# Experts of an early-fusion block: turning and copying the next unit's rows earlier inside a unit

## What is computed

```python
logits = x @ gate_w.T + gate_b
top_vals, top_idx = jax.lax.top_k(logits, TOP_K)          # TOP_K = 2 of 8 experts
routing = jax.nn.softmax(top_vals)
for e in range(E):
    h = x @ w1[e].T + b1[e]                                # 512 -> 1024
    x_glu, x_lin = h[:, 0::2], h[:, 1::2]
    y = x_glu * jax.nn.sigmoid(1.702 * x_glu) * (x_lin + 1.0)
    ye = y @ w2[e].T + b2[e]                               # 512 -> 512
    we = jnp.sum(routing * (top_idx == e), axis=-1)
    out = out + ye * we[:, None]
```

## Time and profile before

| what | value |
|---|---|
| median of 3 runs | 1779.68 us (1773.2 to 1782.53) |
| span of the profiled execution, first to last instruction | 1771.3 us |
| profiled execution's own device time | not listed on its own; the three runs are 1.9 to 11.2 us over the span |
| PE busy over the span | 1334.8 us (75%) |
| DVE, ACT, POOL busy | 1275.3, 774.9, 494.2 us |
| experts, from the first first-product to the last second product | 1295.01 to 1741.85 us of the span, a quarter of it |
| chain that ended last, by line | L1930 16%, L1942 8%, L1914 1% |

### The profile page before, as it was taken

How to read it: one execution, slowest core, us unless ns; L and a number is a source line. 1 busy time by engine, 2 the same in 40 slices (tenths; PEclk the granted TensorE clock), 3 DMA queues, 4 the chain that set the end, 5 groups by cost and what they waited for, 6 DMA issues and landing times. The chain is left out here.

```text
span 1771.3 us, 30260 instructions
## 1 busy us (share of the span) xinstructions
PE 1334.8 (75%) x10236; PEld 761.7 (43%) x10236; DVE 1275.3 (72%) x2068; ACT 774.9 (44%) x1498; POOL 494.2 (28%) x312
## 2 busy tenths in 40 slices
PE   0366447838999999999999922147389999999993
PEld 0335122303444444444444300025367777777772
DVE  7976999968888888888888559998734444444441
ACT  3565313314676767777777710012033333333331
POOL 4000326742333433433200012213012332332321
PEclk9987668857999999999999965666589999999997
DMA  4002016785676677677554334416388878878855
GB/s 150 1 0 68 19 46 206 238 190 141 189 203 190 189 202 200 186 202 204 138 95 80 114 126 85 65 43 188 121 303 274 280 258 269 283 257 266 275 159 143
DMA packets 115662, 294.31 MB, mean 166 GB/s; under 512 B 19772, under 2 KB 54332, under 8 KB 105446
## 3 DMA queue, kind: packets, MB, share of 16 engines
q1 hardware_dynamic: 89262, 205.79, 37.9%
q0 software_dynamic: 25280, 84.95, 18.2%
q10 hardware_dynamic: 1056, 2.79, 0.5%
HBM read 206.39 MB, written 92.16 MB: 169 GB/s over the span
## 5 line engine op out<-in xcount | busy, mean ns | idle before, releaser
L1410 ACT ACTIVATE pT<-p 128x512 f32<-128x512 f32 x800 | 421.1, 607 | 168.1 <-PE p L1312 166.0
L1384 DVE TENSOR_REDUCE mxa<-p 128x1 f32<-128x512 f32 x640 | 409.3, 682 | 96.0 <-PE p L1294 96.0
L1294 PE MATMUL p<-ks,qs 96*128 96x512 bf16 x640 | 252.7, 398 | 32.6 <-DMA vs<-d_v 29.5
L1312 PE MATMUL p<-qs,ks 128*128 128x512 bf16 x640 | 245.0, 383 | 29.6 <-DMA qs<-nmT 17.6
L1330 PE MATMUL p<-pT,vs 128*32 128x128 f32 (+1 forms) x2560 | 205.5, 439 | 1.0 <-ACT pT L1410 1.0
L1930 PE MATMUL p<-x,w 128*128 128x256 bf16 x1728 | 191.6, 273 | 0.0
L1930 PEld LDWEIGHTS p<-x,w 128*128 128x128 bf16 x1728 | 169.1, 98 | 23.4
L1901 POOL DMA_INDIRECT d_acc<-yo,slot_row x54 | 86.6, 1603 | 310.8 <-DMA d_acc<-yo,slot_row 266.1
L2009 DVE SCALAR_TENSOR_TENSOR sg<-p,b,sg 128x256 f32<-128x256 f32 x108 | 52.3, 484 | 118.2 <-ACT sg L1975 118.2
L1330 PEld LDWEIGHTS p<-pT,vs 128*32 128x32 f32 x2560 | 66.8, 109 | 151.2 <-issue 108.4
L1265 POOL CAST xT<-xT 128x2048 bf16<-128x2048 f32 x24 | 45.3, 1887 | 297.9 <-PE p L1330 285.9
(11 more groups left out here) (340 smaller groups left out, 2073.9 us busy)
## 6 DMA issues: line engine op xcount, KB each, us to landing
w<-d_w SPq DMA_DIRECT2D x18, 2048.0 KB, 8.5
d_w<-xT POOLq DMA_DIRECT2D x24, 1024.0 KB, 6.4
shared<-d_w SPq DMA_DIRECT2D x9, 2048.0 KB, 8.5
w<-d_w SPq DMA_DIRECT2D x18, 1024.0 KB, 7.2
xT<-in_w1T POOLq DMA_DIRECT2D x16, 1024.0 KB, 10.7
qs<-d_q SPq DMA_DIRECT2D x192, 80.0 KB, 3.6
ks<-d_k SPq DMA_DIRECT2D x192, 80.0 KB, 3.7
d_v<-xT SPq DMA_DIRECT2D x20, 512.0 KB, 4.4
```

Of the source, the lines that this page charges most:

```text
L1294: mm = pe.matmul(out, qs[u][0:STACK, h, q], ks[u][0:STACK, h, 0:512], start=True, stop=True)
L1312: mm = pe.matmul(out, ks[u][:, h, k], qs[u][:, h, 0:512], start=True, stop=True)
L1384: dve.tensor_reduce(mxa[u][:, h, qt:qt + 1], bank, AX.X, ALU.max, negate=True).then_inc(s_mfree, 1)
L1410: act.activation(dst, ps[:, second_bank(c, s)], ACT.Exp).then_inc(s_p, 1)
```

## The change

`turn` moves to the place behind the second of the four first-product blocks, and `copy_rows` on ACT and DVE to the place behind the third. No instruction's shape, buffer or semaphore changes. The unit that runs last still has no turn.

```diff
@@ tensor
                     mm.then_inc(s_g1, 1)
-                if not last:
-                    turn(i, c + 1)
+                    if o == 1 and not last:
+                        turn(i, c + 1)
                 pe.wait_ge(s_w[c][1], 16 * (i + 1))
@@ scalar
                     act.copy(y[c][:, o, 0], yf[o % 2][:]).then_inc(s_yh, 1)
-                if n + 1 < NU:
-                    copy_rows(n + 1)
+                    if o == 2 and n + 1 < NU:
+                        copy_rows(n + 1)
```

## The result

| | before | changed |
|---|---|---|
| median of 4 runs | 1779.83 us (1773.2 to 1782.53) | 1820.85 us (1817.03 to 1825.42) |
| ratio, 95% interval | | 1.0227 (1.0197 to 1.0258) |
| profiled execution: span | 1771.3 us | 1823.4 us (device time 1825.42) |
| experts, first first-product to last second product | 1295.01 to 1741.85: 446.8 us | 1303.76 to 1793.84: 490.1 us |

The change made the kernel 2.3% slower, some 41 us, where 5 us were forecast; the time lies outside the range. (The two spans are 52 us apart, since the profiled execution was the fastest of its runs before and the slowest after.) Of these 52 us, 43.3 arose in the experts. The other 8.8 are in stages ahead of them, whose code is the same: in the nine profiled executions of this study the experts began between 1295.0 and 1306.4 us, and the one of before is the earliest.

What follows compares the result with a forecast made beforehand. PE was taken as the bound, waiting for nothing at 16.55 us a unit. Late-gather stalls of 1.7, 1.1, 1.0, 0.5 and 0.7 made 5 us, all else 0: 1779.7 + 5 = 1784.7 us, range 1777 to 1800.

Steps and rivals of the forecast that it cites:

- What bounds the kernel; no wait to remove: In the experts PE is busy 429.01 of 429.01 us and waits for nothing, so reordering cannot gain time.
- Copies 0, switches 0: Copies moved on ACT and DVE delay no second products, and one more PE switch per unit costs nothing: 0 us.
- The turn's wait for the gather is the cost, in units at the start and the end: On PE, the earlier turn waits for the next unit's gathered rows in some first and last units: 5 us.
- A few units at the start and some at the end are late, the middle is not: Before any shift, unit 2's gather is 0.8 us late, unit 23's 1.1 late, unit 10's has 0.8 to spare.
- The landing shifts by 0.89 us: First-product weights go out 0.89 us later, so gathers land 0.89 later: units 2, 23, 10 late by 1.7, 2.0, 0.1.
- A stall frees POOL from the weights, so stalls end themselves: Stalls let scatters lead the weights, so gathers go earlier; first units' stalls run 1.7, 1.1, 1.0, 0.5 us.
- The gathers stay late: Rival, chance 0.27: scatters stay behind the weights and the turn waits in every unit, 16 us, 1796 us.
- A stall costs the clock too: Rival, chance 0.08: four stalls each slow PE's next first products by 1.43 us, 5.7 us on top, 1790.4 us.

## Why the prediction was wrong, point by point

- *What bounds the kernel; no wait to remove.* Right: without late rows the time is that of before (ratios 1.0007 and 0.9985).
- *Copies 0, switches 0.* Right, by the run with the turn alone and by the one with the sooner gather, which has the whole change and no loss.
- *The turn's wait for the gather is the cost, in units at the start and the end.* Right in kind. The Trainium skill's rule on issuing early and waiting late (page "DMA: Bandwidth & Descriptors", section "Rules for kernel authors") named the same wait; here it cost 32.2 us of idle time in 16 units, not only at the two ends.
- *A few units at the start and some at the end are late, the middle is not.* The first step that failed, by its reading. Unit 10 alone stood for the middle, with 0.8 us to spare; by the records of landing 12 of the 23 units were late for the new turn without any shift, units 12 to 14 among them. Each landing of before moved by 0.89, and each unit paying anew, gives 23.5 us (an estimate from these records) where the prediction's sum for that rival has 16.
- *The landing shifts by 0.89 us.* A step that failed, a term mis-sized: about 2.8 us with later weights alone. The shift was carried over as a distance. But in most of the middle units the gather of before landed in a gap between two weight transfers of which only the first is moved. In the run with later weights alone the gap is later and about half as long, and in the run with the turn behind the third block the rows land 8.8 us into unit 9. With the transfers apart again they land at 5.8 to 5.9 in units 12 and 13.
- *A stall frees POOL from the weights, so stalls end themselves.* The step that failed by mechanism. Its first half came true: 23 scatters wait for rows instead of 3. But a scatter that waits for rows goes out among the weights as well and takes 9.88 us, where I had it get through ahead of them, and the gather stands behind it on POOL. PE's rows release the scatter, and the scatter holds back PE's gather: a loop of 36.9 us for two units. A long stall did free the next unit, but only that one: behind the 3.35 us in unit 2 the rows for the turn in unit 3 landed 3.3 us ahead of that unit's start, and unit 4 was late by 3.88 again. Take away either side of it, the order on POOL or the weights, and no stall is left.
- *The rivals.* "The gathers stay late" was the outcome by its place and its sign, with another mechanism (POOL held by PE's rows as well as by the weights) and 16 us against 43. "A stall costs the clock too" was true for five stalls and worth 8 us; I had it on top of the forecast and not on top of the late gathers. The Trainium skill's page "TensorE: Matmul & The Clock Gate", section "HAM oscillation — how this bites in real kernels", tells of a kernel in which each wait for DMA between bursts throttles the burst behind; the trace agrees for the stall of 3.35 us (0.78 granted), and behind the one of 1.48 the clock stayed at 1.00.

What stays open is how the 43 us divide between the lost gap, the rows that were late from the start, and the loop, as each feeds the others; putting the gap back won some 18 us. Why some stalls near 2.5 us cost the clock and others did not was not tried: in the run with the turn alone, the unit with a stall of 2.38 us (unit 21) took 1.83 us more than its stall explains, and the one with 2.76 us (unit 11) only the 0.18 that every stall costs.

## What to carry to other kernels

Before a wait is moved ahead, measure when what it waits for arrives, on every unit, and ask what else moves with it: here the same edit drew two transfers together and cut short the gap in which the awaited one had landed. If the awaited transfer is issued behind work that itself waits for this engine, the spare time is not a reserve but one side of a loop, and past zero the loop's own period sets the time. The remedy is to issue the transfer further ahead in its own queue's order, three changed lines here; it made the earlier wait free, and no faster than before.

## What the runs showed of the hardware

- A scatter of 256 KB beside the weights left POOL idle for up to 9.8 us in the changed kernel and 12.1 with all weights in one piece, where without weights it was at most 5.4.
- Weight transfers that were asked for 6.07 us apart left the software queue 86.1% of the engines for about two microseconds between them; 5.1 apart left 52.4% at the same place in a unit, and 86.7% for about one microsecond.
- An idle time of 3.35 us on PE was followed by a granted clock of 0.78 over the next 6.7 us, one of 1.48 by 1.00.
